# Linear-attention key-value sums moved to the start of the kernel, with the first layer norm and the query heads interleaved

## The reference

```python
x = x + xattn0(layernorm(x), ctx)          # softmax attention, 16 heads of 128, 4 key-value heads
x = x + moe0(layernorm(x))                 # 8 experts, top 2, and a shared expert
x = x + xattn1(layernorm(x), ctx, mask)    # linear attention, 16 heads of 16, 64 features
x = x + moe1(layernorm(x))

# xattn0: q = rms_norm(ln(x) @ Wq), 16 heads;  k = rms_norm(ctx @ Wk);  softmax(q k^T) v
# xattn1: k = ctx @ Wk.T + bk;  v = ctx @ Wv.T + bv     (both from the context alone)
k_prime = relu(einsum('bhnd,fd->bhnf', k, Wkf)) * mask
kv      = einsum('bhnf,bhne->bhfe', k_prime, v)       # the key-value sums
k_sum   = sum_n k_prime
out     = (q_prime @ kv) / (q_prime . k_sum)
```

## Time and profile before

| | us |
|---|---|
| median of 3 runs | 1376.37 (1375.21 to 1379.68) |
| profiled execution, device time | 1371.49 |
| its span, first to last instruction | 1369.8 |
| TensorE busy in it | 1215.0 (89%) |
| VectorE, ScalarE, GpSimd busy | 916.7, 740.2, 533.7 |

### The profile page before, as it was taken

The page is one execution under the profiler, slowest core; times in us unless marked ns, Lnnn a source line. Parts: engine busy times, 40 slices in busy tenths (PEclk is TensorE's granted clock), DMA queues, the critical chain, the costliest instruction groups (busy, mean ns, idle before and its releaser), DMA issues. The chain is left out here.

```text
span 1369.8 us, 27004 instructions
## 1 busy us (share of the span) xinstructions
PE 1215.0 (89%) x9559; PEld 1045.8 (76%) x9559; DVE 916.7 (67%) x1895; ACT 740.2 (54%) x1258; POOL 533.7 (39%) x553
## 2 busy tenths in 40 slices
PE   4669999999999999999999578959999999968697
PEld 3448888888887888888888467848888888855586
DVE  6847887878788778888765765346656655653543
ACT  4736666576675666666665215425645555531542
POOL 2636354553636435354451424422122222201442
PEclk9859999999999999999999798979999999988799
DMA  4031111011110101100000600021111111005000
GB/s 150 1 90 46 46 46 46 1 44 45 45 45 15 46 30 45 45 30 15 0 1 1 219 1 1 0 90 43 44 45 44 31 45 45 1 2 210 1 1 14
DMA packets 34205, 57.13 MB, mean 42 GB/s; under 512 B 2802, under 2 KB 29794, under 8 KB 33634
## 3 DMA queue, kind: packets, MB, share of 16 engines
q1 hardware_dynamic: 34146, 56.35, 12.6%
HBM read 55.89 MB, written 0.46 MB: 41 GB/s over the span
## 5 line engine op out<-in xcount | busy, mean ns | idle before, releaser
L711 POOL TENSOR_TENSOR att_sq<-att_work,att_sq 128x500 fp32r<-128x500 f32 x96 | 127.0, 1323 | 178.5 <-DVE att_sq L609 178.5
L716 POOL TENSOR_TENSOR att_k<-att_work,att_k 128x500 fp32r<-128x500 f32 x96 | 129.5, 1349 | 160.0 <-DVE att_k L617 160.0
L98 PE MATMUL att_csum<-att_pT,att_cn 125*128 125x448 f32 x384 | 155.2, 404 | 1.3 <-DVE att_pT L655 0.4
L533 ACT ACTIVATE att_pr<-att_pr,att_nmx 112x1500 f32<-112x1500 f32 (+1 forms) x96 | 108.5, 1131 | 67.7 <-DVE att_nmx L646 67.7
L1469 POOL TENSOR_TENSOR kvs_ct<-kvs_raw,kvs_ct 128x1000 fp32r<-128x1000 f32 x24 | 56.6, 2357 | 223.4 <-ACT kvs_ct L1347 223.4
L100 PE MATMUL att_csum<-att_pT,att_cn 125*128 125x448 f32 x384 | 140.1, 365 | 0.0
L99 PE MATMUL att_csum<-att_pT,att_cn 125*128 125x448 f32 x384 | 139.6, 364 | 0.0
L655 DVE TENSOR_TENSOR att_pT<-att_ring,att_pT 125x448 fp32r<-125x448 f32 x192 | 118.5, 617 | 22.7 <-ACT att_pT L549 22.5
L643 DVE TENSOR_SCALAR_CACHE_REDUCE att_pr<-att_ring 112x500 f32<-112x500 f32 x192 | 120.8, 675 | 4.1 <-PE att_ring L100 2.3
L463 PEld LDWEIGHTS att_ring<-all_ident,att_pr 112*125 112x125 f32 x768 | 110.2, 189 | 14.3 <-ACT att_pr L533 2.2
L1288 PE MATMUL kvs_feat<-kvs_f,kvs_ks 128*125 128x256 f32 x768 | 112.2, 285 | 7.4 <-DVE kvs_kp L1437 5.6
(11 more groups left out here) (254 smaller groups left out, 3312.2 us busy)
## 6 DMA issues: line engine op xcount, KB each, us to landing
att_raw_n<-in_ctx SPq DMA_DIRECT2D x16, 750.0 KB
kvs_raw<-in_ctxT SPq DMA_DIRECT2D x24, 500.0 KB, 3.6
attention_raw_t<-in_ctxT SPq DMA_DIRECT2D x7, 1500.0 KB, 6.2
w_gate<-in_gate SPq DMA_DIRECT2D x1, 2112.0 KB, 8.6
w_up<-in_up SPq DMA_DIRECT2D x1, 2112.0 KB, 13.4
qry_raw<-in_wq SPq DMA_DIRECT2D x4, 512.0 KB, 5.0
wo_raw<-in_wo SPq DMA_DIRECT2D x4, 512.0 KB, 5.7
w_down<-in_down SPq DMA_DIRECT2D x1, 2048.0 KB, 18.4
```

Source lines behind the costliest of these rows:

```text
L98: nc.tensor.matmul(out, w_lo, x_hi, start=start, stop=False, skip_group_check=True)
L533: nc.scalar.activation(pr[:, j, keys], pr[:, j, keys], ACT.Exp, scale=-1.0, bias=nmx[:, j:j + 1], accum_out=z[:, 4 * u + j, c:c + 1]).then ...
L711: nc.gpsimd.tensor_tensor(sq[1][:, i % 2, :], work[:, i % 2, :], sq[0][:, i % 2, :].bitcast(F32), ALU.subtract).then_inc(sq_lo, 1)
L716: nc.gpsimd.tensor_tensor(k[1][x], work[:, i % 2, :], k[0][x].bitcast(F32), ALU.subtract).then_inc(k_lo, 1)
```

## The change

`queries` and `key_value_sums` become one stage, `sums_and_queries`, at the very start; ln0, the clearing of `kvd` and the load of x ahead of everything go away as stages of their own. In the new stage:

- Steps 0 to 7 handle contexts 1 to 7 and then 0, so that the split of context 0 is left in `ct` for the softmax attention (the layouts of `raw_t` and `ct` there become chunk first, and `load_t` three transfers for one).
- Step 0 also holds ln0: its transposes after tile 4, its copies after tiles 5 and 6, and the split of the attention's key and value weights at tiles 9 and 10.
- Steps 1 to 6 hold two query heads each, at tiles 0 and 6; step 7 holds four, at tiles 0, 3, 6 and 9. The square comes one tile after the product, the mean product three (two in step 7) and the root four (two) tiles after.
- Keys and query heads have one PSUM bank each where there were two and four; the sums and their transposes share one. `kp` and `vs` become rings of 6 tiles for 12, and `add` runs every three tiles at tiles 1, 4, 7 and 10.
- The keys of the next chunk are issued at tiles 0 and 2 of a chunk where it was 1 and 2. The split of chunk c + 2 stays at the end of chunk c.
- `kv` (128 x 1088) is kept in a compact form; `linear_readout` clears `kvd` and fills it on GpSimd with two copies, ahead of its `read`. x is loaded again in `attention_output`, where `before` is set too.

In the diff the functions named `step` are TensorE's, ScalarE's and VectorE's, in this order, and the lines with `split_square` are GpSimd's; the last lines are `linear_readout`'s.

```diff
-def queries(nc, xn, qT, wq_dram, qw_dram, kw_dram, splits):
+def sums_and_queries(nc, kv, qT, raw, ct, wk0, wv0, a, ident):
...
+        keys_ps = p.ps("keys_ps", [128, 512])
+        vals_ps = p.ps("vals_ps", [128, 2, 512])
+        feat = p.ps("feat", [128, 2, 512])
+        sums = p.ps("sums", [128, 2, 4 * FD])
+        proj = p.ps("proj", [128, 512])
+        mean = p.ps("mean", [128, 512])
...
+        SQUARE_AT, MEAN_AT, ROOT_AT = 1, {False: 3, True: 2}, {False: 4, True: 2}
...
+        def queries_at(i, first, last, t, after):
+            if first:
+                return []
+            heads = {0: (0, 2 * (i - 1)), 6: (1, 2 * (i - 1) + 1)} if not last else \
+                {3 * n: (n % 2, NH - 4 + n) for n in range(4)}
+            return [heads[t - after]] if t - after in heads else []
...
+            def keys(i, c, m):
+                wait(pe, t_lo, i * KC + c + 1)
+                wait(pe, ks_lo, 4 * (i * KC + c) + 2 * m)
...
+            def features(i, t):
+                for half in range(2):
+                    wait(pe, ks_lo, 4 * (i * KC + c) + 2 * (half + 1))
+                    wait(pe, (kp_low, kp_high)[half], i * KT + t)
...
+            def step(i, first, last):
+                for c, to_project, _ in chunks(i, last):
+                    for n in range(TPC):
+                        t = c * TPC + n
+                        values(i, t)
+                        features(i, t)
+                        if t % GROUP == 1:
+                            if t > 1:
+                                add(i, t // GROUP - 1)
+                            elif not first:
+                                add(i - 1, NG - 1)
+                        if n in (0, 2) and to_project is not None:
+                            keys(*to_project, n // 2)
+                        if t == 2 and not first:
+                            turn(i - 1)
+                        if first and t == 4:
+                            turn_x()
+                        for k, h in queries_at(i, first, last, t, MEAN_AT[last]):
+                            mean_square(h, k)
+                        for k, h in queries_at(i, first, last, t, 0):
+                            project(h, k, i - 1 if not last else h // 2)
...
+            def step(i, first, last):
+                for c, to_project, to_split in chunks(i, last):
+                    for n in range(TPC):
+                        t = c * TPC + n
...
+                        nc.scalar.activation(kp[:, t % RING, 0:512], feat[0:KP, 0, :], ACT.Relu,
+                                             bias=zero[0:KP, 0:1]).then_inc(kp_low, 1)
+                        if t == 2 and not first:
+                            take_sums(i - 1)
+                        if n in (0, 2) and to_project is not None:
+                            keys(*to_project, n // 2)
+                        for k, h in queries_at(i, first, last, t, SQUARE_AT):
+                            square(h, k)
+                        for k, h in queries_at(i, first, last, t, ROOT_AT[last]):
+                            root(h, k)
...
+                        if not last and t == 8:
+                            split_heads(i)
+                    if to_split is not None:
+                        split(*to_split)
...
+            def step(i, first, last):
...
+                        if n in (0, 2) and to_project is not None:
+                            keys(*to_project, n // 2)
+                        if t == 2 and not first:
+                            read_blocks(i - 1)
+                        for k, h in queries_at(i, first, last, t, SQUARE_AT):
+                            round_square(h, k)
+                        for k, h in queries_at(i, first, last, t, ROOT_AT[last]):
+                            normalise(h, k)
+                        if first and t == 0:
+                            sharpen()
...
+                        for k, h in queries_at(i, first, last, t, SQUARE_AT):
+                            split_square(h, k)
+                        if not last and t == 8:
+                            split_heads(i)
+                    if to_split is not None:
+                        split(*to_split)
...
-def key_value_sums(nc, kvd, ctxT_dram, mask_dram, wk_dram, bk_dram, wv_dram, bv_dram, wf_dram, ident):
...
+            nc.gpsimd.memset(kvd[:], 0.0).then_inc(kvd_set, 1)
+            pool.wait_ge(kvd_set, 1)
+            for i in range(2):
+                r = slice(64 * i, 64 * (i + 1))
+                nc.gpsimd.tensor_copy(kvd[r, :, :, RV * i:RV * (i + 1)], kv[r]).then_inc(kvd_done, 1)
```

More of the change, by code:

```diff
@@ new lines, in sums_and_queries, with context, one, chunks @@
+        SQUARE_AT, MEAN_AT, ROOT_AT = 1, {False: 3, True: 2}, {False: 4, True: 2}
+        def context(i):
+            return i + 1 if not isinstance(i, int) else (i + 1) % B
+        def one(n):
+            return slice(n, n + 1) if isinstance(n, int) else bass.ds(n, 1)
+        def chunks(i, last):
+            for c in range(KC):
+                project = (i, c + 1) if c + 1 < KC else (i + 1, 0)
+                split = (i, c + 2) if c + 2 < KC else (i + 1, c + 2 - KC)
+                yield c, None if last and c + 1 >= KC else project, None if last and c + 2 >= KC else split
@@ L206, in _, with load @@
         @block.sync
         def _(sp):
[L208 to L216, removed]
+            def load(i, c):
+                wait(sp, t_lo, (i - 1) * KC + c + 1)
+                src = a["ctxT"][one(context(i)), :, c * CH:(c + 1) * CH]
+                sp.dma_start(raw[:, c], src.rearrange("a (k p) n -> p (a k) n", p=128)).then_inc(loaded[c], 16)
@@ new lines, in add @@
+            def add(i, g):
+                n = i * KT + (g + 1) * GROUP
+                wait(pe, v_set, n)
+                wait(pe, v_mask, n)
+                wait(pe, kp_low, n)
+                wait(pe, kp_high, n)
+                if g == 0:
+                    wait(pe, kv_done, 4 * i)
+                for t in range(g * GROUP, (g + 1) * GROUP):
+                    for r in range(4):
+                        for j in range(4):
+                            h = 8 * (r // 2) + 2 * j + r % 2
+                            last = nc.tensor.matmul(sums[32 * j:32 * j + RV, 0, r * FD:(r + 1) * FD],
+                                                    vs[:, t % RING, h, :], kp[:, t % RING, h * FD:(h + 1) * FD],
+                                                    start=(t == 0 and r == 0), stop=(t == KT - 1 and r == 3),
+                                                    skip_group_check=True)
+                last.then_inc(sums_done, 1)
@@ L225, in mean_square @@
                 for half in (1, 0):
-                    last = nc.tensor.matmul(mean[:, h % 2, 0:NTOK], mean_mat[:], sq[half][:, h % 3, :],
+                    last = nc.tensor.matmul(mean[:, 0:NTOK], mean_mat[:], sq[half][:, k, :],
                                             start=(half == 1), stop=(half == 0))
                 last.then_inc(mean_done, 1)
[L230 to L238, removed]
@@ L242, in _ @@
+            pe.wait_ge(w_lo, 2)
+            for m in range(DC):
+                keys(0, 0, m)
+            pe.wait_ge(f_split, 1)
+            pe.wait_ge(set0, 5)
+            run_peeled(pe, step)
+            add(B - 1, NG - 1)
+            turn(B - 1)
         @block.scalar
         def _(act):
-            nc.scalar.preload_act_table_set(LN_EXP)
[L245 to L266, removed]
@@ new lines, in _ @@
+            act.wait_ge(guess_done, 1)
+            nc.scalar.activation(rstd[:], rstd[:], ACT.Exp, scale=-0.5, bias=zero[0:TP, 0:1]).then_inc(guess_done, 1)
+            act.wait_ge(f_loaded, 16 * 8)
+            nc.scalar.activation(f2[:, 0, :], fmap[:], ACT.Copy).then_inc(f_hi_done, 1)
+            act.wait_ge(const_loaded, 32)
+            for m in range(DC):
+                keys(0, 0, m)
+            split(0, 1)
+            run_peeled(act, step)
+            take_sums(B - 1)
+            act.wait_ge(kv_taken, 4 * B)
@@ L353, in softmax_attention @@
         eps_set = p.sem("eps_set")
-        t_loaded = p.sem("t_loaded")
+        t_loaded = [p.sem(f"t_loaded{c}") for c in range(KC)]
         n_loaded = [p.sem(f"n_loaded{i}") for i in range(2)]
@@ L1546, in read @@
                 wait(pe, qf_done, NH // 2)
+                wait(pe, kvd_done, 2)
                 wait(pe, att_done, b - 1)
```

746 lines of the change are left out of this document (350 added, 396 removed).

## The result

The changed kernel takes **1410.3 us** (median, 1409.37 to 1411.35) against 1375.79 for the kernel before on the same chip: a ratio of 1.0253, interval 1.0218 to 1.0289, so 2.5% slower. The forecast was 1390.4 with a range to 1408, so the sign is right and the size is not: the time lies above the range.

A forecast was written before the change was run, and what follows sets the result against it. TensorE, busy 89% of the span, was taken as the bound. New stage 51 + 6 x 47.4 + 64.8 = 400.2 against 391.8 gives 8.4; clock 5.6; 1376.4 + 14.0 = 1390.4 us, eight-in-ten range 1356 to 1408.

The forecast's parts named there:

- The schedule of a step: Middle loop step of the new first stage: 47.4 us, 37.5 TensorE's own, 9.3 main waits, the rest small waits.
- The named waits: Loop step: keys of tiles 0 and 8 wait 1.7 each, features of tiles 0, 4 and 6 0.7 to 1.3.
- The clock term: New stage's waits at tile 0: one clock fall in two of seven places, 3.5 x 1.6 = 5.6 us.
- my rival with a fall at both places of every step: Loop: clock falls at both long waits of every step, 22 us; 30 slower in all, 1407; chance 0.07.
- 14.0: Whole kernel: forecast slowdown in us, 8.4 from the schedule plus 5.6 from the clock.
- The start: From kernel start to the keys of tile 8 in step 0: 51 us, including 7.3 of waits.
- the place of the keys: Keys behind one tile wait for GpSimd's context split: 1.7 us at tile 0 and 1.75 at tile 8.
- The rival that the waits would melt: ScalarE's chain at tiles 10, 11, 7 and 8: split ready in time, step 39.4, kernel 1335 to 1372; chance 0.25.
- That the heads' weights would be late: Loop steps: the two heads' weights, 256 KB a step, arrive late; chance 0.01.

The follow-up runs named there:

- e8: Changed kernel with context split after a chunk's second tile, root and normalise ahead of the keys' evacuation, sums read at tile 3: 1348.92 us, 0.9809 of the kernel before.
- e6: Changed kernel with the next chunk's keys back at tiles 1 and 2, nothing else undone: 1361.67 us.
- e9: Changed kernel with keys at tiles 1 and 2, root and normalise ahead of the keys' evacuation, sums read at tile 3, split at chunk's end: 1346.72 us.
- e1: Changed kernel with the context split made after the second tile of a chunk instead of at its end, on ScalarE and GpSimd: 1373.2 us.
- e4: Changed kernel with 52 extra unused 256-column matmuls in each loop step, placed where TensorE waits: 1393.92 us.
- e7: Kernel before the change with the next chunk's keys at tiles 0 and 2, nothing else changed: 1398.2 us.
- e5: Changed kernel without its query heads, queries set to zero, so work is missing: 1360.59 us.

## Why the prediction was wrong

**The schedule of a step was nearly right.** I had 37.5 of TensorE's own and 9.9 of waits, 47.4. The same 606 matmuls are busy for 39.6 at full clock (39.66, 39.75 and 39.51 in e8, e6 and e9), and the changed kernel idles 7.8, which adds up to 47.4 as well. The two parts differ from mine by 2: the profile counts a matmul's tail as busy and I worked with starts (eight features last 1.12 in the row at 1034.09 of the earlier trace rows, and the next product starts 0.95 behind them). That the sums agree to 0.1 is luck in part, for the waits were read in steps in which the clock was low. One stretch can be read by starts at full clock, from the keys of tile 8 to those of tile 0:

```profile
105.35 0.49 PE L101 MATMUL kvs_keys_ps<-attention_ct,kvs_wk 128*128 128x500 f32 x1 [1.52 <-POOL attention_ct L659]
...
121.01 0.55 PE L101 MATMUL kvs_keys_ps<-attention_ct,kvs_wk 128*128 128x500 f32 x1 [1.36 <-POOL attention_ct L659]
```

It takes 15.7 where the forecast had 15.3. With 1.6 for 3.4 us at the lower clock (e1), and 6.8 us of it in each step, the whole step would be 48.0 at full clock, an estimate: 0.6 over the forecast. The named waits came at the places named, and none at the keys of tile 4.

**The clock term is the step that failed.** I wrote "one fall in two of seven such places", 5.6 us. In the changed kernel each loop step has 6.8 us at the lower clock: 43.3 busy for 39.6, 3.7 a step, 22 in six. Part of this comes back in waits that get shorter (the keys of tile 0 wait 1.36 where the clock is still up and 1.0 where it is already low), and e1, with most of the waits in place, is busy for 40.0 at full clock, so 22 is an upper bound. e4 gives a lower one, 16, with the extra matmuls' own cost still in it, and e1's price for one fall (1.6, from neighbouring steps) gives 19. So the term was about a third of the real one or less. In size the outcome is near my rival with a fall at both places of every step, 22 and 1407, to which I gave 0.07; in place it is not, since the falls came at three of six and six of six.

My reason for one in two was that of two idle stretches of 2.3 in the query stage one was followed by a fall and one was not the earlier trace rows. I treated them as draws for single waits, and I counted tile 0 alone. In the new step several short waits stand close together. Behind those at tile 0 (1.13, 0.53 and the keys' 1.36) the clock was low in all six steps, in three of them from before the third wait on; behind those of tile 6 (1.12, 0.60) in three of six. The Trainium skill, "TensorE: Matmul & The Clock Gate", section "Part 1: The HAM clock gate", makes the slow clock the default. By that rule the forecast put the term at 11: still below all three figures, but nearer than mine. The runs bear the rule out only in part, since in e6 no fall followed such waits in the loop.

**Where the difference between 14.0 and 38.2 comes from.** Between the spans of the two profiled executions it is 24.1, and these parts add up to it within the rounding:

- The six steps, 22.4 less the 5.6 already allowed for the clock: 16.8. By the figures above some 10 to 16 of it is the clock, and the rest the schedule.
- The start, keys of tile 8 in step 0 at 53.1 for 51: 2.1. The clock is low there from 25.7 to 29.1, and the forecast had no fall at the ends.
- From the keys of tile 8 in step 6 (359.95) to the attention, 68.7 for 64.8: 3.9. The clock is low for 6.8 from 373.9 on, some 3.1 by e1's price.
- From ln2's start to the end, 148.2 for 145.5: 2.6. The clock is low for 45.8 us in it where it was for 43.1, which explains up to 1.3. 1.1 arises behind moe1's last VectorE work, in the store. The cause of the rest stays open.
- ln2 1.48 behind moe0 for 1.3: 0.2.
- Attention to moe0, 829.6 for 831.2: 1.6 less, with 65.0 us at the lower clock for 70.4.

**What the waits hang on.** The forecast priced the place of the keys by GpSimd's split alone, 3.5 of a step. e6 shows that the place is worth 6.8 (3.3 less idle, and 3.6 less busy since the clock stays up): the split, the evacuations that lose their cover (e7 shows these alone, 2.9 a batch), and through both the clock. The heads are worth 6.9 by e5. The two figures can't be added, since each edit alone also brings the falls down (to none in e6's loop, to one in five of the six steps in e5). The rival that the waits would melt is out: each wait came at its place, up to 0.4 shorter than forecast (0.7 where the clock was low). That the heads' weights would be late is out too: no projection in the loop waits for anything.

## What to carry to other kernels

Interleaving a stage whose engines wait for one another with a TensorE-bound one can pay (e9 is 2% faster than the kernel before, and its work is the changed kernel's), but the order in the evacuating engines' queues decides it: put a product that needs evacuation where the next product of another kind covers it, and an operation with slack behind the ones that a bank waits for, not ahead. Price a position twice, by what it must wait for and by what its evacuation then holds back. And when TensorE's waits stop being one long stretch and become several short ones close together, give the case of a fall at each such place real weight: the clock fell behind 9 of 12 such places in this loop and behind 2 of 12 in e1's. Where the waits can't go, filling them is worth a test.

## What was not expected of the hardware

Waits as short as 1.12 and 0.60, with 0.7 of work between, were followed by 3.4 us at 1.2 GHz (196.4 to 199.8). But the same pair isn't followed by the same thing each time: in e1 1.13 and 0.53 at 199.67 and 200.91 were (the clock is low for 3.4 from 201.6 on), and 1.13 and 0.53 at 291.31 and 292.55 were not; in e6 the pair of 1.13 and 0.52 never was in the loop. What decides between them these runs don't show. Filling the waits with 52 unused matmuls a step made a kernel with more work 16 us faster.
